# A convolution, MLP and convolution kernel: setup order, the first image's squares, and loads in the MLP's tail

## The reference, cut to what matters

```python
y = depthwise_conv(x, dw_w, 7x7, pad 3) + dw_b          # first stage
y = layernorm_over_channels(y) * ln_w + ln_b            # statistics at the end of the first stage
h = gelu(y @ w1 + b1)                                   # 96 -> 384, per pixel
gx = sqrt(sum over the pixels of one image of h*h)      # GRN: needs the whole image
nx = gx / (mean over hidden units of gx + 1e-6)
z = x + (grn_gamma * h * nx + grn_beta + h) @ w2 + b2   # 384 -> 96
z = clip(floor(z * 65536) / 65536)                      # fixed point
out = depthwise_conv(z, sign and power of two of cw, 3x3, pad 1) + fixed_point(cb)
```

## Time and profile before

| | us |
|---|---|
| median of 3 runs | 1080.11 (1079.97 to 1080.11) |
| the profiled execution | 1080.37 |
| its span on the core | 1078.6 |
| PE busy in it | 990.8 (92%) |
| DVE busy | 825.5 (77%) |
| ACT busy | 830.8 (77%) |
| POOL busy | 411.7 (38%) |

### The profile page before, as it was taken

The page is one execution under the profiler, slowest core; times in us unless marked ns, Lnnn a source line. Parts: engine busy times, 40 slices in busy tenths (PEclk is TensorE's granted clock), DMA queues, the critical chain, the costliest instruction groups (busy, mean ns, idle before and its releaser), DMA issues.

```text
span 1078.6 us, 21092 instructions
## 1 busy us (share of the span) xinstructions
PE 990.8 (92%) x5574; PEld 717.7 (67%) x5574; DVE 825.5 (77%) x1768; ACT 830.8 (77%) x1724; POOL 411.7 (38%) x353
## 2 busy tenths in 40 slices
PE   3999999999999467999999999999999849999996
PEld 2788888888888355666666666666666427767774
DVE  7777777777777565888888888888887667888885
ACT  2688888888887357898988888888888607787874
POOL 2666676666666153332333333333332001111110
PEclk9999999999999766999999999999999978999999
DMA  8777777777772592555555555555543247999995
GB/s 162 147 183 182 181 179 184 187 187 179 180 179 66 131 225 82 157 175 163 172 162 171 172 162 170 162 171 162 167 136 90 80 110 187 245 248 243 247 244 154
DMA packets 146312, 182.95 MB, mean 170 GB/s; under 512 B 13799, under 2 KB 140424, under 8 KB 143208
## 3 DMA queue, kind: packets, MB, share of 16 engines
q1 hardware_dynamic: 145480, 179.97, 62.5%
q10 hardware_dynamic: 800, 2.61, 1.0%
HBM read 124.28 MB, written 58.25 MB: 169 GB/s over the span
## 4 chain that ended last, share of the span: by engine, by line
PE 71%; DVE 12%; ACT 6%; issue 6%; DMA 3%; DVEq 1%; POOL 0%; ACTq 0%; SPq 0%; POOLq 0%
PE psum L573 22%; PE psum L653 21%; PE psum L643 6%; PE psum L644 6%; PE psum L645 6%; PE psum L552 6%; PE psum L600 3%; DVE arena_r L894 3%; ACT arena L706 2%; ACT arena_r L691 2%; DVE arena L919 1%; DMA arena<-lines_a 1%; DVE arena L923 1%; DVE arena L1079 1%; DVE arena L1068 1%
## 5 line engine op out<-in xcount | busy, mean ns | idle before, releaser
L573 PE MATMUL psum<-arena_r 112*128 112x464 f32 x1536 | 375.2, 386 | 0.3 <-issue 0.2
L573 PEld LDWEIGHTS psum<-arena_r 112*128 112x128 f32 x1536 | 276.8, 190 | 33.9 <-issue 1.1
L653 PE MATMUL psum<-arena,w2s 128*96 128x448 f32 x672 | 266.8, 542 | 2.8 <-DVE w2s L994 2.8
L787 ACT ACTIVATE arena<-psum,b1g 128x448 f32<-128x448 f32 x336 | 201.8, 630 | 58.3 <-PE psum L645 58.2
L497 POOL TENSOR_TENSOR arena_r<-arena,arena_r 96x448 fp32r<-96x448 f32 x112 | 134.1, 1197 | 268.7 <-DVE arena_r L969 194.8
L653 PEld LDWEIGHTS psum<-arena,w2s 128*96 128x96 f32 x672 | 109.8, 164 | 119.1 <-issue 111.8
L643 PE MATMUL psum<-arena_r,w1h 96*128 96x448 f32 x336 | 154.1, 459 | 14.2 <-POOL arena_r L497 13.0
L706 ACT ACTIVATE arena<-psum,bias_a 64x224 f32<-64x224 f32 (+1 forms) x288 | 117.0, 442 | 61.8 <-PE psum L573 50.6
L894 DVE TENSOR_TENSOR arena_r<-psum,arena_r 112x224 fp32r<-112x224 f32 x384 | 127.2, 382 | 48.3 <-ACT arena_r L691 47.5
L691 ACT ACTIVATE arena_r<-psum 112x224 fp32r<-112x224 f32 x384 | 112.6, 355 | 54.8 <-PE psum L552 52.5
L486 POOL TENSOR_TENSOR arena<-arena 128x448 f32<-128x448 f32 x96 | 110.0, 1146 | 109.8 <-DVE arena L923 109.2
(11 more groups left out here) (94 smaller groups left out, 1146.1 us busy)
## 6 DMA issues: line engine op xcount, KB each, us to landing
arena<-lines_a SPq DMA_DIRECT2D x48, 448.0 KB
arena<-in_x_dram SPq DMA_DIRECT2D x48, 392.0 KB
y_scratch<-arena SPq DMA_DIRECT2D x48, 392.0 KB
arena<-in_x_dram SPq DMA_DIRECT2D x112, 168.0 KB, 2.5
z_scratch<-arena SPq DMA_DIRECT2D x112, 168.0 KB, 2.0
arena<-z_scratch SPq DMA_DIRECT2D x48, 392.0 KB
out_dram<-arena SPq DMA_DIRECT2D x48, 392.0 KB
arena_r<-y_scratch SPq DMA_DIRECT2D x98, 168.0 KB, 2.6
```

Source lines behind the costliest of these rows:

```text
L573: mm = nc.tensor.matmul(p_conv[s % 2][:, 0:NCOL], w[:, p, s, TW * k:TW * k + TW], v[:, p, s, slot0 + k:slot0 + k + JP, :].rearrange("p j i ...
L653: mm = nc.tensor.matmul(p_o[k][0:C, 0:CH], w2s[:, p, m, :], hid[:, p, m, CH * t:CH * t + CH], start=(m == 0), stop=(m == MT - 1))
L787: nc.scalar.activation(hid[:, p, m, CH * t:CH * t + CH], p_h[m][:, 0:CH], ACT.Gelu, bias=b1g[:, m:m + 1]).then_inc(gelu_done, 1)
```

## The change

The setup loads are split: the two conv weights and the biases go on ACT's queue with semaphores of their own (`c_in`, `bias_in`, `small_in`), and ACT runs one small activation before it waits. The first rows are loaded in two halves around the storing of the lines. The filter lines are written by one strided copy each. The first batch's tables come one channel at a time, each with its semaphore. PE waits per channel for high and low tables. DVE's work on the last stage's filter and bias moves ahead of the first batch. In the first batch, the next one's rows and tables are prepared one channel later (`AHEAD0`). The transposes back use 56 rows and columns in place of 64. The first stage stores two batches back.

In the MLP, four of the first image's squares and one of the last image's go to DVE; the first image's down projection runs three chunks behind, with the GRN sum one chunk later. `hid` becomes two tiles, so that the even one's memory is free in the tail. There SP loads, for two batches of the last stage, the rows of images 0 to 13 and the tables; images 14 and 15 follow when z is stored. POOL clears the halos.

```diff
+AHEAD0 = ((), (0, 1), (2,), (3,))
+FIRST_LEAD = 3
...
-    return bass.AP(tensor=v.tensor, offset=v.offset + LSTEP - 1,
-                   ap=[part, [LSTEP, n], [bank, 2], [-1, W]])
+    return bass.AP(tensor=v.tensor, offset=v.offset + W - 1,
+                   ap=[part, [W, n], [bank, 2], [-1, W]])
...
+        hid0 = mlp(128, MT, HW)
         ct = mlp(C, 2, CH)
         xr = mlp(C, HW)
-        hid = mlp(128, 2, MT, HW)
...
+        hid = [hid0, mlp(128, MT, HW)]
+        sqv = mlp(128, SQ_WIDE)
...
+        def by_vector(i, m, part):
+            return isinstance(i, int) and (i == 0 and (part == 0 or m == 0) or i == NIMG - 1 and part == 1 and m == 0)
...
+            half_rows(0)
             sp.wait_ge(lines_made, 1)
             store_lines(lines_a, la, zrow, KA)
+            half_rows(1)
             sp.wait_ge(lines_out, 3 * 16)
...
-                            if ahead:
-                                tables(b + 1, 1 - s)
-                        if not ahead:
-                            tables(b, s)
-                        if not (isinstance(b, int) and b < 3):
-                            store(b - 3, 1 - s)
+                            tables(b + 1, 1 - s)
+                        if not (isinstance(b, int) and b < lag):
+                            store(b - lag, (s + lag) % 2)
...
-            tables_a(0, 0)
-            conv_transfers(stages["a"], x_v, y_v, tables_a, True)
+            for k in range(CB):
+                for r in range(2):
+                    shifted = bass.AP(tensor=lines_a, offset=k * (KA * TW) + LPAD + r * LSTEP - (W - 1), ap=[[1, W], [1, KA * TW]])
+                    sp.dma_start(toep[W * r:W * r + W, 0, k, :], shifted).then_inc(t_first[k], 16)
+            load_rows(stages["a"], x_v, 1, 1)
+            tables_a(1, 1)
+            for dst, src in ((w1r, w1),
+                             (w2r[:, :, :], w2.rearrange("(t p) c -> p t c", p=128))):
+                sp.dma_start(dst, src).then_inc(small_in, 16)
+            conv_transfers(stages["a"], x_v, y_v, tables_a, 2)
...
+            sp.wait_ge(o_done, NCH * (NIMG - 1))
+            for k in range(4):
+                sp.wait_ge(z_out[k], 16 * Z_USES[k % 2] * (NIMG // 2 - 1))
+            for b in range(2):
+                first_rows(b, 0, NI2 - 1, c_early[b])
+                tables_c(b, b)
             step(NIMG, 0, more_y=False, more_x=False)
...
-            load_rows(stages["c"], z_v, 0, 0)
-            sp.wait_ge(halo, 2)
-            conv_transfers(stages["c"], z_v, out_v, tables_c, False)
+            for b in range(2):
+                first_rows(b, NI2 - 1, NI2, stages["c"][f"x{b}"])
+            conv_transfers(stages["c"], z_v, out_v, tables_c, 3)
...
-                        if S is stages["a"]:
-                            pe.wait_ge(S["tl"], CB * b + CB)
...
+                        if w is toep_l and k == 0:
+                            pe.wait_ge(S["tl"], channel + 1)
...
-                            mm = nc.tensor.transpose(outs[s % len(outs)][0:CM, 1 - r, LSTEP * n:LSTEP * n + LSTEP],
-                                                     yt[q:q + LSTEP, p, i, (h + 1 - r) % 2].rearrange("p g m -> p (g m)"),
-                                                     ident[q:q + LSTEP, q:q + LSTEP])
+                            mm = nc.tensor.transpose(outs[s % len(outs)][0:CM, 1 - r, W * n:W * n + W],
+                                                     yt[q:q + W, p, i, (h + 1 - r) % 2].rearrange("p g m -> p (g m)"),
+                                                     ident[q:q + W, q:q + W])
...
-            pe.wait_ge(v_ready, NCH * NIMG)
-
...
-            for dy in range(7):
-                for dx in range(7):
-                    at = (dy + 1) * LSTEP + dx - 3
-                    ins = dve.tensor_copy(la[:, at:at + 1], wa[:, 7 * dy + dx:7 * dy + dx + 1])
+            dve.tensor_copy(taps[:, :, 0:7], wa.rearrange("p (y x) -> p y x", y=7)).then_inc(lines_made, 1)
...
+            def squares(i, p, m, part):
+
+                t0, t1 = ((0, SQ_SPLIT), (SQ_SPLIT, NCH))[part]
+                dve.wait_ge(gelu_done, MT * (NCH * i + t1 - 1) + m + 1)
+                need(dve, sq_dve, vector_squares[0])
+                v = hid[p][:, m, CH * t0:CH * t1]
+                dve.scalar_tensor_tensor(out=sqv[:, 0:CH * (t1 - t0)], in0=v, scalar=1.0, in1=v, op0=ALU.mult, op1=ALU.mult,
+                                         accum_out=ss[:, p, m, part:part + 1]).then_inc(sq_dve, 1)
...
+                    normalise(1, 1, 0)
+                    for m in range(MT):
+                        squares(0, 0, m, 0)
+                    normalise(1, 1, 1)
+                    squares(0, 0, 0, 1)
+                    grn_sums(0, 0)
+                    normalise(1, 1, 2)
+                    return
+                if fixed and i == 1:
+                    grn_scale(0, 0)
+                    for t in range(3, NCH):
                         normalise(1, 1, t)
```

More of the change, by code:

```diff
@@ L214, in build @@
         small_in = sem("small_in")
+        c_in = sem("c_in")
+        bias_in = sem("bias_in")
         dw_in = sem("dw_in")
+        t_first = [sem(f"t_first{k}") for k in range(CB)]
         consts = sem("consts")
@@ L233, in build @@
         m2_done = sem("m2_done")
+        c_early = [sem(f"c_early{b}") for b in range(2)]
         var_ready = sem("var_ready")
@@ L481, in add @@
                     if not (last and p == 1):
-                        for q in AHEAD[s]:
+                        for q in (AHEAD0 if first and p == 0 else AHEAD)[s]:
                             table_low(b + 1, q, 1 - p)
@@ L502, in step @@
                 for t in range(NCH):
-                    if t == NCH - 1 and not (fixed and i == NIMG):
+                    if t == (2 if fixed and i == 0 else NCH - 1) and not (fixed and i == NIMG):
                         pool.wait_ge(ss_ready, i + 1)
@@ L659, in step @@
                 head, tail = fixed and i == 0, fixed and i == NIMG
-                for t in range(NCH + LEAD):
+                lead = FIRST_LEAD if fixed and i == 1 else LEAD
+                for t in range(NCH + lead):
                     if t < NCH and not tail:
                         up(i, p, t)
-                    if t == 0 and not head:
+                    if t == (1 if fixed and i == 1 else 0) and not head:
                         pe.wait_ge(gx_ready, i)
@@ L724, in conv_stage @@
                 for s in range(G):
+                    if rows_too and s == G - 1:
+                        table_high(0, 0, 0)
                     xt_copy(0, s, 0)
                 if rows_too:
-                    for s in range(CB):
+                    for s in range(1, CB):
                         table_high(0, s, 0)
@@ L777, in step @@
                 tail = fixed and i == NIMG
-                need(act, o_done, NCH * (i - 1))
+                if not tail:
+                    need(act, o_done, NCH * (i - 1))
                 for t in range(NCH):
@@ L868, in setup @@
-                link(dve.tensor_tensor(bias_c[:, :], bq[1], bq[0], ALU.add))
                 dve.tensor_scalar(w1g, w1r, lnw[:, 0:1], None, ALU.mult).then_inc(w1_made, 1)
@@ L1041, in step @@
                 for t in range(NCH):
+                    last_image = fixed and i == NIMG - 1
                     if t == NCH - 1 and not tail:
+                        if last_image:
+                            squares(i, p, 0, 1)
                         grn_sums(i, p)
```

182 lines of the change are left out of this document (104 added, 78 removed).

## The result

The kernel after takes 1070.84 us (median of 4 runs, 1068.66 to 1071.91), the kernel before 1080.11 beside it. The ratio is 0.9904, 95% interval [0.9892, 0.9917]. The forecast was 1062.2 in a range of 1055 to 1069: the direction holds, the size does not, 9.3 us gained of 18. Timed again later, it gave 1071.51 against 1080.67, ratio 0.9916 [0.9899, 0.9933].

What follows compares the result with a forecast made beforehand. The prediction took TensorE, with 71% of the chain, as the bound, so edits pay where it stands still or loses work; 6.3 + 1.5 + 5.7 + 4.5 = 18.0 us gave 1062.2 us, range 1055 to 1069.

Steps and rivals of the forecast that it cites:

- Which stage is bound by what: Whole kernel: TensorE bounds the stages' middles; it waits at start, setup's end, first image's end and passage to last stage.
- Start, 6.3: First stage's opening: earlier lines and tables bring the low part after finish_setup forward, gain 6.3 us, bounds 4.7 and 8.5.
- second tables near 21.9: First stage's opening: the second batch's tables arrive near 21.9 us, against 26.59 before.
- finish_setup ... starts near 36.1: First stage, batch 1: VectorE's low_part after finish_setup starts near 36.1 us, against 42.45 before.
- Transposes, 1.5: First and last stages: transposes of 56 for 64 rows and columns gain 1.5 us, bounds 0 and 3.9.
- Store lag, 0: First stage: storing two batches back, not three, costs 0, any slight table lateness being covered by ACT's spare time.
- Rival (d): First stage: the burst behind the later store sets the pace, each of 20 batches 0.9 us longer; 1083, chance 0.03.
- no ACT wait for tables: First stage: a sign that batches run 13.8 to 13.9 us apart without ScalarE waiting for tables.
- First image, 5.7: MLP's first image: squares moved to VectorE and a later down projection gain 5.7 us, bounds 3.5 and 7.
- rival (b): First image: squares cost double, 15 us, sums start at 415, no gain there; 1067.9 or 1070, chance 0.12.
- Passage, 4.5: MLP to last stage: early loads bring the convolution to 887.1 despite a 3.3 us VectorE stand; gain 4.5 us.
- Rival (a): Tail of the MLP: stores are not held up and VectorE never waits; 1058.6, chance 0.14.

Runs made afterwards that it cites:

- both mended: Kernel after plus eight unread matmuls behind the second image's first up projection, and its fourth chunk's normalisation ahead of the GRN scale: 1067.62 us.
- The pair of 1058.42 and 1062.95: Kernel after with one early last-stage batch, old order there, first-image edits, w1g and setup finish reordered: 1058.42 us; same without eight extra first-image matmuls: 1062.95.

## Why the prediction was wrong

- **Which stage is bound by what**: right. What was gained or lost lies at the four places named but for 1.2 us along the first stage and 0.4 in the last, and the steady batches stayed at 13.88.
- **Start, 6.3**: 3.3 in the profiled run, 5.1 in the mean of nine. The step "second tables near 21.9", and with it "finish_setup ... starts near 36.1", was too early by 2.5 and 1.7; in nine traces the tables came at 22.4 to 24.4. The rest is the clock, which the forecast never followed here: with w1g as late but the wait filled, batch 2 came 2.5 us sooner.
- **Transposes, 1.5**: 0.9 by the stages, 1.5 by the medians [0.1, 2.4]. Near enough.
- **Store lag, 0**: 0.4, once, and not in every trace. Rival (d) is out: no steady batch became longer. But the forecast's sign "no ACT wait for tables" did not hold: behind the 2.4 us at the start ScalarE waits ten times more for tables, 3.7 us in all and 0.9 at most. With stores three back only the wait at the start is left. ScalarE's spare time covered them, as the forecast argued.
- **First image, 5.7**: 0.9 to 1.6. This is the term that failed most. The squares took 2.0, 2.8, 2.0 and 1.6 us and the sums came on time, so rival (b) is out; 0.8 us of the 2.8 is the only slowing. The failed steps, in the time of before (with the head start of 4.2 added): up(1,1) was to start at 408.2 and end by 411.5, and went from 409.6 to 413.1 at half clock, with the GRN matmul behind it; "w2s is ready near 413" was 415.3; "up(1,3) ends near 417.7" was 421.3. The forecast let "by PE's clock" into one up alone, where the second, third and fourth up and the first down ran at half clock, and it names no wait of TensorE for the fourth normalisation, which stands behind the scale. With both mended the place gives 6.9 us (58.7 - 51.8), more than the forecast wanted. Its sign "the first down near 418" is met by 417.12 only because that time leaves the head start out; with it 413.5 was due.
- **Passage, 4.5**: 4.9 up to the first convolution, stand 3.8 for 3.3. Rival (a) is out. But the sum lacked a term: the new order of preparations applies in the last stage's first batch too, and takes 2.0 to 2.6 us back.
- **The sum**: profiled, 3.3 - 0.3 (lag) + 1.2 (the rest of the first stage, 0.6 of it in step with the batches) + 1.6 + 4.9 - 2.6 + 0.4 = 8.5, the difference of the spans.

I priced each stall by its length, and what it leaves behind, a slower TensorE for the next microseconds, in one place only. Three things stay open: why the second tables land up to 2 us apart in the same opening, the 0.6 us by which the start is late even with its wait filled, and how often an execution falls on which side.

## What to carry to other kernels

A wait of TensorE costs its length and, where the clock falls with it, the matmuls that run at half clock behind it; look at the granted clock in the windows after each stall, and ask whether an edit moves the stall or removes it. When work moves to another engine, follow the queue of the engine that receives it to the next thing that TensorE needs: here one normalisation behind a scale was worth 2.6 us. An order chosen for one stage that a shared loop applies to another must be costed there as well. And two edits of one place must be run together before their gains are added: here one of them asked for rows that the other had made late.

## What the runs showed of the hardware

- One and the same opening came out at 48.66 or at 52.02 us at batch 2. The trace with TensorE standing 2.48 us had a granted clock of 0.56 behind it; of two that stood 0.98, one had 1.00 and one 0.72. The Trainium skill ("TensorE: Matmul & The Clock Gate", Part 1: The HAM clock gate) says that the clock has two rates and is chosen by how busy the engine has been of late. The pair of 1058.42 and 1062.95 agrees: only eight filler matmuls differ, and the clock in 400 to 410 us is 1.00 with them and 0.66 without.
- Full clock gave 0.20 us from one 448-column matmul to the next, half clock 0.37.
- VectorE's square over 128x1792 took 2.0 us and over 128x1344 1.55. The second of the four took 2.8, in all thirteen traces that have it: it alone began while a POOL subtraction was under way. The first and the fourth began 0.16 us ahead of one and were not slowed; the subtractions themselves then took 2.87 and 2.38 us, where 1.44 is usual here. That POOL is the cause was not tested by moving it.
- A 168 KB store behind 1.86 MB of loads of the same queue took 7.6 us to land, where 2.0 is usual.
